# Second cross attention of a two-layer decoder: scores in half bursts, six turned tiles, the output product in four parts, late queries projected early

## The chip, the cores and the metric

The kernel runs on one core of one Trainium2 chip. The metric is the device time of one launch in microseconds; the time before is the median of three runs. The engines are TensorE (PE, with its weight loads PEld), VectorE (DVE), ScalarE (ACT), GpSimd (POOL) and SyncE (SP), which issues the loads. Each works through its own queue in order and meets the others only at semaphores.

## The reference

x is (8, 128, 512) in fp32 and passes six sublayers, each as `x = x + f(layernorm(x))`: a Taylor-like product with an FFN, a cross attention of 32 heads of 128, a LoRA FFN, a linear attention, the grouped cross attention that is changed here, and a 3-bit dequantised linear layer. The fifth is:

```
q = (queries @ Wq).reshape(b, s, KV_HEADS, GROUP, HEAD_DIM)     # 8 x 4 heads of 16
k = (keys @ Wk).reshape(b, s, KV_HEADS, HEAD_DIM)
v = (values @ Wv).reshape(b, s, KV_HEADS, HEAD_DIM)
scores = jnp.einsum('bqhgd,bkhd->bhgqk', q, k) * scale
attn = jax.nn.softmax(scores, axis=-1)
out = jnp.einsum('bhgqk,bkhd->bqhgd', attn, v).reshape(b, s, EMBED)
return out @ Wo
```

## The kernel before

Everything stays in SBUF between sublayers. Projections are written as three products of split operands (`mm3`, lines 542 to 544: high by high, low by high, high by low). The order on every engine is written out by hand.

The changed stage is the fifth sublayer. Its 8 batches times 8 key heads are worked in 16 groups n = 0 to 15 (`NG`), two per batch (b = n // 2, part = n % 2). A group has four tiles g = 0 to 3 (`KG`); each holds 4 heads of 128 queries by 128 keys, one PSUM bank of 128x512. Banks are sc0, sc1, pj0, pj1 for scores, tp and ou1 for turned tiles, pv for the heads' output and ou0 for projections and output products. For one group:

- `scores(n)` on PE (line 969): 8 matmuls with 32 rows each, tile g on rows 32g to 32g+31, so that four row groups work side by side.
- `row_max(n, g)` on DVE (line 1938), then `exps(n, g)` on ACT (line 1320, four ACTIVATEs), then `row_sums(n, g)` on DVE (lines 1945, 1948: a sum and a reciprocal), then `normalise` on POOL (line 514).
- `transposes(n, g)` on PE (line 983) turns the tile into tp or ou1; `turned_out(n, g)` on ACT (line 1329) copies it to `turned_whole` (`TW`, four tiles before).
- `values(n)` on PE (line 997) multiplies the four turned tiles with the values into pv. After the second group of a batch `heads(b)` takes pv to `act_hi` (ACT, line 1335) and `act_lo` (DVE, line 1954), `output(b)` on PE multiplies with Wo in four chunks (12 matmuls into ou0), and `add(b)` on DVE (lines 1397 and 1960) adds to x and takes the statistics.

`queries(hf, c)` projects four batches' queries for one of four column blocks: 12 matmuls into a bank and a copy on ACT (line 1312). Half 0 is done ahead of the groups. Half 1 goes through bank ou0 behind the groups 5, 6 and 7 (one, one and two blocks), because its result is written over that of half 0 in `act_whole` (`AF`).

`exps(n+1, g)` writes over the tile that `transposes(n, g)` reads (`PR[:, g]`). Before, ACT takes group n's turned tiles 0, 1 and 2 first and only then starts the exps of group n+1; `turned_out(n, ·)` waits for `values(n-1)`, since there are four turned tiles. DVE also has four parts of a dequantisation (`dequantise`, lines 1514 to 1518) for the last layer in its queue, ahead of group 0 and in groups 0, 1 and 3. POOL's order (`block_keys`, `pad_values`, four `normalise`) is not touched.

Of the kernel before, what the change touches and what calls it, by code (L numbers as in the profile page):

```python
# [17 lines left out]
FP32 = mybir.dt.float32  # L18
# [7 lines left out]
P = 128  # L26
# [63 lines left out]
NG = B * KVH // KG  # L90

# [17 lines left out]
def build(nc, a):  # L109
    ctx = ExitStack()  # L110
    with ctx:
# [33 lines left out]
        with ExitStack() as shared:  # L145
            TW = shared.enter_context(nc.sbuf_tensor("turned_whole", [P, KG, 512], FP32))
# [165 lines left out]
        query_banks = [ou[0], ou[1], pv, ou[0]]  # L312

# [224 lines left out]
        def _(pe):  # L538
# [398 lines left out]
            def queries(hf, c):  # L937
# [18 lines left out]
            def scores(n):  # L956

                b, part = n // 2, n % 2
                pe.wait_ge(kx_ready, n + 1)
                pe.wait_ge(q_out, b // HB * KC + 2 * part + 2)  # L960
                if n:
                    pe.wait_ge(lx_exp, n * KG)
                else:
                    pe.wait_ge(pj_done, PJ["ln4"] + B)
                for h in range(2):
                    for g in range(KG):
                        r = slice(32 * g, 32 * g + 32)
                        at = (2 * part + h) * HALF + b % HB * S
                        last = pe.matmul(score_banks[g][:, h * 256:(h + 1) * 256], AF[r, at:at + S], KX[r, n % 2, :],  # L969
                                         start=True, stop=True)  # L970
# [15 lines left out]
            def values(n):  # L986
# [8 lines left out]
                for g in range(KG):  # L995
                    at = part * P + 32 * g
                    last = pe.matmul(pv[32 * g:32 * g + 32, :], pads(b)[:, at:at + 32], TW[:, g, :],
# [3 lines left out]
            def output(b):  # L1001
                pe.wait_ge(on_done, b + 1)
                pe.wait_ge(x_done, OU["l1x"] + b)
                pe.wait_ge(q_out, 4 if b < 2 else 5 if b == 2 else 8)
                if b == 0:
                    ready(4, SLOT["l1x"][4])
                    ready(3, SLOT["l1x_o"])
                for c in range(KC):
                    last = mm3(ou[0][:], both(A, lambda t: t[:, ON1 + c * P:ON1 + (c + 1) * P]),
                               wrows(WO_SLOTS)(c), c == 0, c == KC - 1)  # L1010
                last.then_inc(ou_full, 1)
# [30 lines left out]
            scores(0)  # L1042
            queries(0, 3)
            for n in range(NG):
# [1080 lines left out]
```

## Time and profile before

| | |
|---|---|
| median of three runs | 2455.73 us (2455.06 to 2457.9) |
| the profiled execution: time, span | 2459.67 us, 2457.8 us |
| stage of the groups, first score to last `values` | 2266.4 to 2421.3 us of the span |
| PE, DVE, ACT, POOL busy in that stage of 154.9 us | 124.4, 114.6, 110.7, 78.0 us |

### The profile page before, as it was taken

To read this page: it belongs to the slowest core of one execution; us is meant where nothing else is said; L and a number is where in the kernel's file an instruction comes from. 1 tells how busy PE (TensorE), PEld (TensorE's weight loads), DVE (VectorE), ACT (ScalarE), POOL (GpSimd) and SP (SyncE) were. 2 spreads that over 40 slices of the span, in tenths; PEclk is the share of its full clock that TensorE was granted. 3 is DMA by queue.
4 is the path that set the end of the run, shared out by engine and by line. 5 is a ranking of instruction groups with operands and counts; after the bars stand their busy time and mean duration, and the time that the engine had idled before them with its cause. 6 is when DMAs were issued, how large, how long until landed. Compare 5 with 4: busy or idle time off the path is not lost.

```text
span 2457.8 us, 38454 instructions
## 1 busy us (share of the span) xinstructions
PE 2358.6 (96%) x13227; PEld 2012.9 (82%) x13227; DVE 1255.9 (51%) x2921; ACT 902.7 (37%) x2232; POOL 668.3 (27%) x383
## 2 busy tenths in 40 slices
PE   4999899999999999998999999999999999998788
PEld 3788688888888888987888888888888888887455
DVE  6444644444444444446554444444444444457766
ACT  2111344444444444443233333333333333334764
POOL 4334522322222232221231111111111111112542
PEclk9999999999999999999999999999999999999889
DMA  3110211211111111110111111111111111110000
GB/s 117 63 48 26 103 52 51 78 58 51 68 51 51 65 71 51 51 68 27 45 54 45 45 45 44 38 40 37 37 38 43 45 45 45 45 54 1 1 1 35
DMA packets 36832, 118.97 MB, mean 48 GB/s; under 512 B 4905, under 2 KB 7337, under 8 KB 36785
## 3 DMA queue, kind: packets, MB, share of 16 engines
q1 hardware_dynamic: 36784, 118.35, 14.1%
q8 instruction: 28, 0.46, 0.1%
q14 instruction: 20, 0.16, 0.0%
HBM read 116.24 MB, written 2.10 MB: 48 GB/s over the span
## 4 chain that ended last, share of the span: by engine, by line
PE 88%; DVE 5%; issue 3%; POOL 2%; ACT 1%; SPq 0%; DMA 0%; POOLq 0%; ACTq 0%; DVEq 0%
PE pj L542 19%; PE pj L543 19%; PE pj L544 19%; PE ou L542 6%; PE ou L544 6%; PE ou L543 6%; PE pv L720 2%; PE sc L857 2%; PE pv L866 2%; PE sc L704 2%; PE tp L711 1%; POOL w_lo L410 1%; POOL w_hi L408 1%; PE sc L969 1%; DVE neg_max L1938 1%
## 5 line engine op out<-in xcount | busy, mean ns | idle before, releaser
L402 POOL TENSOR_TENSOR w_lo<-raw,w_hi 128x1024 fp32r<-128x1024 f32 x145 | 346.7, 2391 | 1441.2 <-ACT w_hi L1104 1401.8
L542 PE MATMUL pj<-xt_hi,w_hi 128*128 128x512 f32 x1232 | 499.8, 406 | 6.6 <-DVE xt_lo L1473 2.4
L543 PE MATMUL pj<-xt_lo,w_hi 128*128 128x512 f32 x1232 | 483.1, 392 | 0.0
L544 PE MATMUL pj<-xt_hi,w_lo 128*128 128x512 f32 x1232 | 482.3, 392 | 0.0
L542 PEld LDWEIGHTS pj<-xt_hi,w_hi 128*128 128x128 f32 x1232 | 233.5, 190 | 51.1 <-issue 3.1
L542 PE MATMUL ou<-w_hi,act_hi 128*128 128x512 f32 x684 | 274.5, 401 | 0.8 <-DVE x L1397 0.6
L544 PEld LDWEIGHTS pj<-xt_hi,w_lo 128*128 128x128 f32 x1232 | 232.6, 189 | 49.7
L544 PE MATMUL ou<-w_hi,act_lo 128*128 128x512 f32 x684 | 267.6, 391 | 0.0
L543 PEld LDWEIGHTS pj<-xt_lo,w_hi 128*128 128x128 f32 x1232 | 233.6, 190 | 40.9
L543 PE MATMUL ou<-w_lo,act_hi 128*128 128x512 f32 x684 | 266.9, 390 | 0.0
L1397 DVE TENSOR_TENSOR x<-x,ou 128x512 f32<-128x512 f32 x192 | 130.8, 684 | 247.1 <-PE ou L544 246.8
L1255 ACT ACTIVATE side<-pj 128x512 f32<-128x512 f32 (+1 forms) x256 | 125.6, 491 | 341.1 <-PE pj L544 341.1
L1835 DVE TENSOR_TENSOR queries_keys<-side,pj 128x512 f32<-128x512 f32 x128 | 88.1, 688 | 184.6 <-ACT side L1255 184.6
L1170 ACT ACTIVATE queries_keys<-pj 128x512 f32<-128x512 f32 x128 | 76.5, 598 | 247.7 <-PE pj L544 247.7
L542 PE MATMUL pj<-w_hi,xt_hi 128*128 128x256 f32 (+1 forms) x544 | 160.8, 295 | 2.5 <-DVE x_sum L1475 1.6
L1104 ACT ACTIVATE w_hi<-raw 128x1024 fp32r<-128x1024 f32 x146 | 153.5, 1052 | 20.5 <-PE ou L544 18.7
L542 PEld LDWEIGHTS ou<-w_hi,act_hi 128*128 128x128 f32 x684 | 128.7, 188 | 36.6 <-issue 10.7
L544 PE MATMUL pj<-w_hi,xt_lo 128*128 128x256 f32 (+1 forms) x544 | 157.4, 289 | 0.0
L543 PE MATMUL pj<-w_lo,xt_hi 128*128 128x256 f32 (+1 forms) x544 | 157.3, 289 | 0.0
L544 PEld LDWEIGHTS ou<-w_hi,act_lo 128*128 128x128 f32 x684 | 128.7, 188 | 27.8
L543 PEld LDWEIGHTS ou<-w_lo,act_hi 128*128 128x128 f32 x684 | 129.0, 189 | 24.3
L542 PE MATMUL pj<-w_hi,ctx_hi 128*128 128x256 f32 x512 | 147.8, 289 | 0.7 <-POOL w_lo L410 0.7
(242 smaller groups left out, 4538.9 us busy)
## 6 DMA issues: line engine op xcount, KB each, us to landing
raw<-in_l1a_w SPq DMA_DIRECT2D x80, 512.0 KB, 4.1
raw<-in_l0x_w SPq DMA_DIRECT2D x64, 512.0 KB, 4.3
side<-in_side SPq DMA_DIRECT2D x32, 512.0 KB, 4.0
raw<-in_ffn_w SPq DMA_DIRECT2D x15, 512.0 KB, 3.3
raw<-in_l0f_w SPq DMA_DIRECT2D x6, 512.0 KB, 3.7
raw<-in_l1x_w SPq DMA_DIRECT2D x6, 512.0 KB, 3.8
raw<-in_taylor_w SPq DMA_DIRECT2D x5, 512.0 KB, 6.9
x<-in_x SPq DMA_DIRECT2D x2, 1024.0 KB, 6.4
```

The source lines that it names most:

```text
L402: pool.tensor_tensor(WL[:, s, :], RAW[:, s, :], f32(WH[:, s, :]), ALU.subtract).then_inc(w_ready[s], 1)
L542: pe.matmul(out, wh, xh, start=first, stop=False)
L543: pe.matmul(out, wh, xl, start=False, stop=False)
L544: return pe.matmul(out, wl, xh, start=False, stop=last)
L704: last = pe.matmul(score(j)[:, h * S:(h + 1) * S], heads_of(0, h, j), heads_of(1, h, j), start=True, stop=True)
L720: last = pe.matmul(pv[:, h * S:(h + 1) * S], VT[:, n, h * S:(h + 1) * S], TA[:, n % 2, h * S:(h + 1) * S], start=True, stop=True)
L857: last = pe.matmul(score(j)[:, h * S:(h + 1) * S], heads_of(1, h, j), heads_of(0, h, j), start=True, stop=True)
L1104: act.activation(WH[:, s, :], RAW[:, s, :], ACT.Copy).then_inc(w_hi[s], 1)
L1170: act.activation(QK[:, n, :], bank[:], ACT.Copy, scale=S ** -0.5 if n < 2 else 1.0).then_inc(pj_done, 1)
L1255: act.activation(F[:, x % 2, 0:w], pj[bank][:, 0:w], ACT.Sigmoid).then_inc(la_sg, 1)
L1397: dve.tensor_tensor(dst, dst, ou[bank][:], ALU.add).then_inc(x_done, 1)
L1835: dve.tensor_tensor(dst, F[:, x % 2, 0:w], pj[bank][:, 0:w], ALU.mult).then_inc(pj_done, 1)
```

## The change

`scores(n, two)` now issues the tiles 0 and 1, or 2 and 3: two bursts of 4 matmuls with two row groups each, each waiting for its own two exps of the group before. PE sends the first half of group n+1 ahead of `transposes(n, 0)` and the second behind `transposes(n, 1)`. `values(n-1)` moves into group n, behind its first turning. `TW` has six tiles (`NTW`), so `turned_out` waits for a `values` less often. `output(b)` is issued in four chunks: the first at the end of the even group 2b+2, the others in group 2b+3 between turnings. ACT alternates `exps(n+1, g)` and `turned_out(n, g)`. DVE takes `row_max(n+1, 0)` and `(n+1, 1)`, then `row_sums(n, 2)` and `(n, 3)`, then the other two maxima, then `row_sums(n+1, 0)` and `(n+1, 1)`. Half 1 of the queries goes to its own place (`RAWF`, two weight slots that are free by then), blocks 0 to 3 ahead of group 0, behind groups 0 and 1, and inside group 4. No instruction's shape changes, and the number of matmuls is the same.

```diff
+NTW = 6
-            TW = ... sbuf_tensor("turned_whole", [P, KG, 512], FP32))
+            TW = ... sbuf_tensor("turned_whole", [P, NTW, 512], FP32))
+        RAWF = RAW[:, 0:2, :].rearrange("p s n -> p (s n)")
+        QUERIES = [AF, RAWF]
...
-                if n in (4, 5):
-                    pe.wait_ge(x_done, OU["l1x"] + n - 2)
-                if n in (6, 7):
+                if n in (4, 5, 6):
                     pe.wait_ge(q_out, n)
+                if n == 7:
+                    pe.wait_ge(x_done, OU["l1x"] + 1)
...
-            def scores(n):
+            def scores(n, two):
                 b, part = n // 2, n % 2
-                pe.wait_ge(kx_ready, n + 1)
-                pe.wait_ge(q_out, b // HB * KC + 2 * part + 2)
+                if two == 0:
+                    pe.wait_ge(kx_ready, n + 1)
+                    pe.wait_ge(q_out, b // HB * KC + 2 * part + 2)
                 if n:
-                    pe.wait_ge(lx_exp, n * KG)
-                else:
+                    pe.wait_ge(lx_exp, (n - 1) * KG + 2 * two + 2)
+                elif two:
                     pe.wait_ge(pj_done, PJ["ln4"] + B)
                 for h in range(2):
-                    for g in range(KG):
+                    for g in (2 * two, 2 * two + 1):
...
             for n in range(NG):
+                late = n % 2 and n > 1
+                if n + 1 < NG:
+                    scores(n + 1, 0)
                 transposes(n, 0)
+                if n:
+                    values(n - 1)
+                if late:
+                    output(n // 2 - 1, (1,))
                 transposes(n, 1)
+                if n == 4:
+                    queries(1, 3)
                 if n + 1 < NG:
-                    scores(n + 1)
+                    scores(n + 1, 1)
+                if late:
+                    output(n // 2 - 1, (2,))
                 transposes(n, 2)
+                if late:
+                    output(n // 2 - 1, (3,))
                 transposes(n, 3)
                 if n % 2 == 0 and n:
-                    output(n // 2 - 1)
-                if n + 1 == NG:
-                    turned_weights(0)
-                    turned_weights(1)
-                values(n)
-                for c in {5: (0,), 6: (1,), 7: (2, 3)}.get(n, ()):
-                    queries(1, c)
+                    output(n // 2 - 1, (0,))
+                if n in (0, 1):
+                    queries(1, n + 1)
+            turned_weights(0)
+            turned_weights(1)
+            values(NG - 1)
...
             def turned_out(n, g):
                 t = n * KG + g
                 act.wait_ge(tn_full, t + 1)
-                if n:
-                    act.wait_ge(pg_full, n)
-                act.activation(TW[:, g, :], turn_banks[t % 2][:], ACT.Copy).then_inc(tn_out, 1)
+                if t >= NTW:
+                    act.wait_ge(pg_full, (t - NTW) // KG + 1)
+                act.activation(TW[:, t % NTW, :], turn_banks[t % 2][:], ACT.Copy).then_inc(tn_out, 1)
...
             for n in range(NG - 1):
+                exps(n + 1, 0)
                 turned_out(n, 0)
+                if n in (1, 2):
+                    queries(1, n)
+                exps(n + 1, 1)
                 turned_out(n, 1)
-                if n == 6:
-                    queries(1, 0)
+                if n % 2 == 0 and n:
+                    heads(n // 2 - 1)
+                exps(n + 1, 2)
                 turned_out(n, 2)
...
             for n in range(NG - 1):
-                for g in range(KG):
-                    row_max(n + 1, g)
+                row_max(n + 1, 0)
+                row_max(n + 1, 1)
+                row_sums(n, 2)
+                row_sums(n, 3)
+                row_max(n + 1, 2)
+                if n % 2 == 0 and n:
+                    heads(n // 2 - 1)
+                row_max(n + 1, 3)
                 if n in (0, 1, 3):
                     dequantise((0, 1, 3).index(n) + 1)
                 row_sums(n + 1, 0)
                 row_sums(n + 1, 1)
-                if n % 2 == 0 and n:
+                if n % 2 and n > 1:
                     add(n // 2 - 1)
...
```

**PE, an odd group.** Before, from the `values` of an even group to the `values` of the odd group behind it: pv is `values`, tp and ou from identity are the four turnings, sc and pj from `keys_blocked` the scores of the group that follows.

```order
L997 MATMUL pv<-turned_whole,values_padded 32x512 x4
L983 MATMUL tp<-identity,probs 128x128 x4
L983 MATMUL ou<-identity,probs 128x128 x4
L969 MATMUL sc<-keys_blocked,act_whole 128x256 x2
L969 MATMUL pj<-keys_blocked,act_whole 128x256 x2
...
L983 MATMUL tp<-identity,probs 128x128 x4
L983 MATMUL ou<-identity,probs 128x128 x4
L997 MATMUL pv<-turned_whole,values_padded 32x512 x4
```

After, the same group: sc and pj are the two half bursts, ou from `w_hi` and `w_lo` one chunk (three matmuls) of the output product.

```order
L974 MATMUL sc<-keys_blocked,raw 128x256 x4
L988 MATMUL tp<-identity,probs 128x128 x4
L1002 MATMUL pv<-turned_whole,values_padded 32x512 x4
L546 MATMUL ou<-w_hi,act_hi 128x512
L547 MATMUL ou<-w_lo,act_hi 128x512
L548 MATMUL ou<-w_hi,act_lo 128x512
L988 MATMUL ou<-identity,probs 128x128 x4
L974 MATMUL pj<-keys_blocked,raw 128x256 x4
...
L988 MATMUL tp<-identity,probs 128x128 x4
...
L988 MATMUL ou<-identity,probs 128x128 x4
```

The `values` product and a chunk now stand between the first and the second turning, so between the first turning and the second half of the next scores.

**ACT, the pass of an even group.** Before: `turned_whole` are the copies of turned tiles, `probs` the exps (x8 is two tiles).

```order
L1329 ACTIVATE turned_whole<-tp 128x512
L1329 ACTIVATE turned_whole<-ou 128x512
L1329 ACTIVATE turned_whole<-tp 128x512
L1320 ACTIVATE probs<-sc,neg_max 128x128 x8
L1329 ACTIVATE turned_whole<-ou 128x512
L1320 ACTIVATE probs<-pj,neg_max 128x128 x8
```

After, with `heads` (`act_hi` from pv) in it:

```order
L1339 ACTIVATE probs<-sc,neg_max 128x128 x4
L1348 ACTIVATE turned_whole<-tp 128x512
L1339 ACTIVATE probs<-sc,neg_max 128x128 x4
L1348 ACTIVATE turned_whole<-ou 128x512
L1354 ACTIVATE act_hi<-pv 128x512
L1339 ACTIVATE probs<-pj,neg_max 128x128 x4
L1348 ACTIVATE turned_whole<-tp 128x512
L1339 ACTIVATE probs<-pj,neg_max 128x128 x4
L1348 ACTIVATE turned_whole<-ou 128x512
```

The exps of the next group no longer stand behind three turned tiles of this one; `heads` moved from the odd group's pass to the next even group's, behind two exps and two copies.

On DVE, `heads` (`act_lo`) moved with it: it now has the maximum of tile 3, and so an exp, queued behind it, where before it stood between the last two row sums.

## Rows read from the trace of the kernel before

**Rows 1.** The page: span, and the granted clock in 40 slices.

```profile
span 2457.8 us, 38454 instructions
...
PEclk9999999999999999999999999999999999999889
```

**Rows 2.** Waits from 2266.4 to 2421.3 us: total, times, longest.

```profile
DVE neg_max L1938 <- PE pj L969: 24.8, 10, 7.9
...
PE pv L997 <- ACT turned_whole L1329: 19.2, 8, 2.8
```

**Rows 3.** DVE timeline, first row maxima of groups 1, 5, 9 and 15.

```profile
2277.58 1.29 DVE L1938 TENSOR_REDUCE neg_max<-sc 128x4 f32<-128x512 f32 x2 [1.10 <-PE pj L969]
...
2315.50 1.29 DVE L1938 TENSOR_REDUCE neg_max<-sc 128x4 f32<-128x512 f32 x2 [2.04 <-PE pj L969]
...
2358.98 1.29 DVE L1938 TENSOR_REDUCE neg_max<-sc 128x4 f32<-128x512 f32 x2 [7.92 <-PE pj L969]
...
2410.78 1.29 DVE L1938 TENSOR_REDUCE neg_max<-sc 128x4 f32<-128x512 f32 x2 [1.27 <-PE pj L969]
```

**Rows 4.** PE timeline, last late query to the values of group 9.

```profile
2354.00 0.50 PE L542 MATMUL ou<-xt_hi,w_hi 128*128 128x512 f32 x1 [0.69 <-ACT act_whole L1312]
...
2356.85 0.60 PE L983 MATMUL tp<-identity,probs 128*128 128x128 f32 x4
...
2357.82 0.48 PE L969 MATMUL sc<-keys_blocked,act_whole 32*128 32x256 f32 x2
...
2358.89 0.65 PE L983 MATMUL tp<-identity,probs 128*128 128x128 f32 x4
2359.38 0.60 PE L983 MATMUL ou<-identity,probs 128*128 128x128 f32 x4
2359.74 0.48 PE L542 MATMUL ou<-w_hi,act_hi 128*128 128x512 f32 x1
...
2362.78 1.06 PE L997 MATMUL pv<-turned_whole,values_padded 128*32 128x512 f32 x8
...
2370.34 1.94 PE L997 MATMUL pv<-turned_whole,values_padded 128*32 128x512 f32 x8 [2.24 <-ACT turned_whole L1329]
```

**Rows 5.** ACT timeline, group 9.

```profile
2367.14 0.60 ACT L1329 ACTIVATE turned_whole<-tp 128x512 f32<-128x512 f32 x1 [1.38 <-PE tp L983]
2367.63 2.17 ACT L1320 ACTIVATE probs<-sc,neg_max 128x128 f32<-128x128 f32 x8
...
2372.34 0.60 ACT L1335 ACTIVATE act_hi<-pv 128x512 fp32r<-128x512 f32 x1 [1.02 <-PE pv L997]
```

**Rows 6.** DVE timeline: a part of the dequantisation, then the add and two row sums.

```profile
2307.82 0.42 DVE L1514 TENSOR_SCALAR w<-w_bytes 128x512 f32<-128x512 uint8 x1
...
2309.61 0.68 DVE L1945 TENSOR_REDUCE row_sums<-probs 128x4 f32<-128x512 f32 x1
...
2363.09 0.66 DVE L1397 TENSOR_TENSOR x<-x,ou 128x512 f32<-128x512 f32 x1
...
2364.39 0.67 DVE L1945 TENSOR_REDUCE row_sums<-probs 128x4 f32<-128x512 f32 x1
...
2365.19 0.65 DVE L1945 TENSOR_REDUCE row_sums<-probs 128x4 f32<-128x512 f32 x1
```

**Rows 7.** POOL timeline, two tiles.

```profile
2365.35 2.04 POOL L514 TENSOR_TENSOR probs<-probs,row_recip 128x512 f32<-128x512 f32 x2 [0.97 <-DVE row_recip L1948]
```

**Rows 8.** Windows: length, busy PE, PEld, DVE, ACT, POOL, granted clock.

```profile
2366.20:2369.60 3.40, 1.31 (x8) 0.84 (x8) 3.24 (x6) 2.46 (x9) 1.76 (x3) 1.00 0.01 2
2369.60:2376.40 6.80, 6.06 (x33) 3.29 (x34) 3.57 (x9) 4.32 (x13) 4.53 (x5) 0.50 0.00 0
2376.40:2386.70 10.30, 8.31 (x60) 5.43 (x59) 9.73 (x19) 8.37 (x28) 5.37 (x8) 1.00 0.01 2
...
2359.00:2410.80 51.80, 42.99 (x277) 25.87 (x278) 40.61 (x82) 38.87 (x123) 28.55 (x33) 0.80 0.01 1
```

**Rows 9.** ACT and PE timelines: the last early query, the last values.

```profile
2270.70 0.60 ACT L1312 ACTIVATE act_whole<-ou 128x512 f32<-128x512 f32 x1 [0.72 <-PE ou L544]
...
2421.20 1.06 PE L997 MATMUL pv<-turned_whole,values_padded 128*32 128x512 f32 x8
```

More of the change, by code:

```diff
@@ L996, in values, with output @@
                     at = part * P + 32 * g
-                    last = pe.matmul(pv[32 * g:32 * g + 32, :], pads(b)[:, at:at + 32], TW[:, g, :],
+                    last = pe.matmul(pv[32 * g:32 * g + 32, :], pads(b)[:, at:at + 32], TW[:, (n * KG + g) % NTW, :],
                                      start=part == 0, stop=part == 1)
                 last.then_inc(pg_full, 1)
[L1001 to L1008, printed above, removed]
+            def output(b, chunks):
+                if chunks[0] == 0:
+                    pe.wait_ge(on_done, b + 1)
+                    pe.wait_ge(x_done, OU["l1x"] + b)
+                    pe.wait_ge(q_out, 8 if b else 7)
+                    if b == 0:
+                        ready(4, SLOT["l1x"][4])
+                        ready(3, SLOT["l1x_o"])
+                for c in chunks:
                     last = mm3(ou[0][:], both(A, lambda t: t[:, ON1 + c * P:ON1 + (c + 1) * P]),
                                wrows(WO_SLOTS)(c), c == 0, c == KC - 1)
-                last.then_inc(ou_full, 1)
+                if chunks[-1] == KC - 1:
+                    last.then_inc(ou_full, 1)
             def product(b):
@@ L1061, in _ @@
             turn(5, range(2))
-            output(B - 1)
+            output(B - 1, range(KC))
             for b in range(B):
@@ L1308, in queries @@
                 act.wait_ge(q_full, n + 1)
-                if hf:
-                    act.wait_ge(gs_full, (7 + c // 2) * KG)
                 bank = ou[0] if hf else query_banks[c]
-                act.activation(AF[:, c * HALF:(c + 1) * HALF], bank[:], ACT.Copy, scale=HD ** -0.5).then_inc(q_out, 1)
+                act.activation(QUERIES[hf][:, c * HALF:(c + 1) * HALF], bank[:], ACT.Copy, scale=HD ** -0.5).then_inc(q_out, 1)
             def exps(n, g):
@@ L1346, in _ @@
                 exps(0, g)
+            queries(1, 0)
             for n in range(NG - 1):
+                exps(n + 1, 0)
                 turned_out(n, 0)
+                if n in (1, 2):
+                    queries(1, n)
+                exps(n + 1, 1)
                 turned_out(n, 1)
-                if n == 6:
-                    queries(1, 0)
+                if n % 2 == 0 and n:
+                    heads(n // 2 - 1)
+                exps(n + 1, 2)
                 turned_out(n, 2)
-                exps(n + 1, 0)
-                exps(n + 1, 1)
+                if n == 4:
+                    queries(1, 3)
+                exps(n + 1, 3)
                 turned_out(n, 3)
-                exps(n + 1, 2)
-                if n % 2:
-                    heads(n // 2)
-                exps(n + 1, 3)
-                if n == 6:
-                    queries(1, 1)
-                if n == 7:
-                    queries(1, 2)
-                    queries(1, 3)
             turned_out(NG - 1, 0)
@@ L1964, in _ @@
                 row_max(0, g)
-            for g in range(KG):
-                row_sums(0, g)
+            row_sums(0, 0)
+            row_sums(0, 1)
             dve.wait_ge(w_hi[3], SLOT["l1x_o"] + 1)
@@ L1975, in _ @@
                 row_sums(n + 1, 1)
-                if n % 2 == 0 and n:
+                if n % 2 and n > 1:
                     add(n // 2 - 1)
-                if n + 2 == NG:
-                    half_deviation(5, 0)
-                row_sums(n + 1, 2)
-                if n % 2:
-                    heads(n // 2)
-                row_sums(n + 1, 3)
+            half_deviation(5, 0)
+            row_sums(NG - 1, 2)
+            row_sums(NG - 1, 3)
+            add(B - 2)
             def weights_lo(c):
```

11 lines of the change are left out of this document (6 added, 5 removed).

## The prediction

> **What bounds the kernel now.** The page first: PE is granted nearly its full clock, but 0.8 in two of the last three slices, 2273 to 2396 us [rows 1]. That is the changed stage, so only its 154.9 us are at stake. In the table of waits of this stage no engine is the bound: DVE waits for scores (24.8 us), PE for turned tiles (19.2 us) [rows 2]. It is a ring: scores, maximum, exps, sum, normalise, turn, copy, values, and back. The pace is best read from the first row maximum of a group: groups 1, 5, 9 and 15 begin at 2277.58, 2315.50, 2358.98 and 2410.78 [rows 3]. I call what lies between the first maximum of group n+1 and that of group n+2 pass n; it is pass n of the loops in the code. Passes 0 to 3 take 37.9 us, 4 to 7 43.5 us (they hold the late queries), 8 to 13 51.8 us, 17.3 us for each pair (one batch). From the maximum of group 15 to its values it is 2421.20 - 2410.78 = 10.4 us [rows 3, 9].
>
> Then the clock. In a stretch of 3.40 us PE works 1.31 us and waits; behind it the grant is 0.50 (1.2 GHz) for 6.8 us, in which a values product takes 1.94 us, where one at the full clock takes 1.06 [rows 4, 8]. Over passes 8 to 13 the mean grant is 0.80 [rows 8]. A fall stands behind the long wait (2.24 us for `turned_out`), once a pair.
>
> **Prices at the full clock.** All from starts in a row. PE [rows 4]: whole burst to the next turning 1.07 (2357.82 to 2358.89), and to the maximum that it releases 1.16 (2358.98 in [rows 3]); a turning 0.5; values 1.0; output product 3.04, so a chunk 0.76, which I take as 0.9 when it stands alone between others; a query block 2.85. ACT [rows 5]: copy 0.5, exps of a tile 1.0 (2.17 with its tail for two), `heads` 0.5. DVE: maximum 0.6 (1.29 with its tail for two [rows 3]); a row sum with its reciprocal 0.8 to 0.9, 0.89 taken; add and statistics 2364.39 - 2363.09 = 1.3; a dequantisation part 2309.61 - 2307.82 = 1.8 [rows 6]; `heads` 0.7, as other subtractions of this size. POOL: 1.0 a tile, with 0.1 to the turning [rows 7].
>
> A half burst is in no row. Its bounds are 0.43 (cost by the number of matmuls) and 0.86 in the array plus the 0.2 of a change of form (cost by the longest row group, since each row group still has the same matmuls in series). I take the upper one, 1.07 and 1.16, because four row groups ran side by side in the row. The Trainium skill says the same in "TensorEngine Tiling (Array Packing)", Theoretical Speedup: a dimension of 32 gives up to four times, which half bursts use half of, and by it PE's scores of a group double. By the lower bound instead the sum below would be some 3 us better.
>
> **An even pass after the change**, from its start at 0. DVE: two maxima to 1.2, two sums to 3.0, third maximum to 3.6. `heads` on DVE waits for ACT: exps from 0.7, copy, exps, copy to 3.7, `heads` done 4.3. DVE goes on to 5.0, last maximum 5.6, two sums 7.4. PE's first chunk and the next first half burst end before that (3.3 and 4.3 for the last turnings, chunk from 5.1, burst from 6.0, maximum possible at 7.15). So 7.4 us, 0.7 of it a wait that the moved `heads` makes.
>
> **An odd pass**, with 0 where the even one ends. The sum of tile 0 ended at -0.9; POOL is done with it at 0.3, turning 0.3, values 0.8 to 1.8, chunk to 2.7, second turning to 3.2, second half burst, third maximum at 4.4. DVE has been idle since 3.0. Then two maxima, two sums, the add: 4.4 + 1.2 + 1.8 + 1.3 = 8.7. A pair is 7.4 + 8.65 = 16.05 us (DVE alone has 14.0: eight maxima 4.8, eight sums 7.1, `heads` 0.7, add 1.3). PE is then idle for at most 1.1 us at a stretch in steady passes, so I take the full clock throughout.
>
> **The sum.**
> - Passes 8 to 13: 3 x 16.05 = 48.15 against 51.8: **-3.6**.
> - Start: the copy of query block 3 is done at 2271.2 (2270.70 + 0.5 [rows 9]). Late block 0 follows on PE to 2273.9, its scores give the first maximum at 2275.05 (2277.58 before). Passes 0 and 1 have a dequantisation on DVE and end in a query block on PE: sums to 3.0, POOL to 4.2, last turning 4.7, block to 7.5, scores 8.65 (DVE alone would need 7.8); pass 1 the same with 0.1 for the values, 8.8. Pass 2 is an even one whose `heads` is 0.5 later, behind the copy of a query block: 7.9. Pass 3 is an odd one with a dequantisation: 8.65 + 1.8. 2275.05 + 8.65 + 8.8 + 7.9 + 10.45 = 2310.85, against 2315.50: **-4.65**.
> - Passes 4 to 7: pass 4 has late block 3 between turning and half burst: it moves the third maximum from 3.0 to 5.4, and PE's first chunk waits for its copy, so 10.2; the others 8.65, 7.4, 8.65. Together 34.9 against 43.5: **-8.6**. Before, three of four query blocks stood bare in passes 5 to 7 (behind the last two DVE had been idle for 7.9 us [rows 3]); now their passes are the ones that DVE's dequantisations fill.
> - The end: before, one output product was over before the last group's turnings, now three chunks stand between them, and they don't overlap with scores any more. From the last maximum of [rows 3]: 7.7 turning, values 9.2, chunk and turning 10.6, chunk 11.5, turning, chunk 12.9, turning 13.4, weights' turnings, values at 14.4 against 10.4: **+4.0**. Behind it the same work follows as before.
> - The larger `TW`, the other place for queries and the waits that are left out add no instruction: 0. Their cover is that ACT has 12.4 us of work in a pair (eight exps 8, eight copies 4, `heads` 0.5); without it an exp's start would move, but DVE sets the pace.
>
> -3.6 - 4.65 - 8.6 + 4.0 = -12.9 us. The profiled execution took 2459.67 us, its span 2457.8, which would become 2444.9; the median of the runs is 3.9 below that time, and -12.9 from 2455.73 gives **2442.8 us**.
>
> **The rivals.** I call no change what lies within 0.2% (4.9 us), about what a measurement of this kernel can tell.
>
> 1. *The low clock comes back, and PE now stands in the ring (ends slower).* In an odd pass, turning, values, chunk, turning and half burst lie one behind the other, 0.5 + 1.0 + 0.9 + 0.5 + 1.16 = 4.1 us, and at 0.50 of the clock 7.8. A fall in each of seven pairs costs 7 x 3.7 = 26 us and gives 2469; it decides at the fourth (12.9 / 3.7 = 3.5). For it: gaps remain (0.9 and 0.5 between turnings in an even pass, up to 1.1 behind a half burst). Against: the fall in the rows stands behind a wait of 2.24 us and one stretch of 3.40 us with 1.31 busy, and the 10.3 us with PE busy 8.31 kept their clock [rows 4, 8]; the new passes have 12 of 16 us busy. One to three falls: 2446 to 2454, 13 in 100; four or more: 2457 to 2469, 14 in 100. The Trainium skill speaks for it in "TensorE: Matmul & The Clock Gate", A second HAM failure mode: frequent small idle spells between groups of matmuls make the clock oscillate. The trace agrees so far that the clock of this stage swings.
> 2. *Little of it arrives.* At the full clock the old order is not much worse: its even leg (9.8 us) would be 8.3 with the 1.5 us of slow values, turnings and scores taken out, so a pair 15.9. What the new order gives is a kept clock and hidden queries. If handoffs that I laid back to back slip by 0.5 us in every pass, 15 x 0.5 takes 7.5 us back: 2450. Between 2450.8 and 2460 for this reason: 7 in 100.
> 3. *The ring opens further.* If a half burst costs 0.43 and the chunk hides, only DVE is left: 14.0 a pair, 2 us better on seven pairs, 2429. Unlikely, since `heads` waits for ACT however fast PE is: 6 in 100.
> 4. The forecast, 2437 to 2449: 60 in 100.
>
> **How the numbers follow.** Forecast and rival 3 and most of the light form of rival 1 are faster by over 0.2%: 0.74. Within 0.2%: the rest of it, rival 2, and the beginning of the heavy form: 0.14. Slower: 0.12. The range of 8 in 10 leaves out rival 3's lower part and the heavy form of rival 1: 2435 to 2456.
>
> **What would show it.** Right: the first maximum of group 15 near 2394, pairs of 16 us, granted clock near 1.0 in the stage, a DVE wait for `act_hi` of 0.7 in even passes and one for scores of 1.4 in odd ones, the last values 14 us behind the maximum. A half burst's eight records would have four starts 0.21 us apart. Wrong: a grant of 0.50 in odd passes, pairs above 17.3, or PE waiting over 2 us for turned tiles.

## The result: 0.4% faster, near the forecast

| | median (lowest to highest, runs) | ratio to before, 95% interval |
|---|---|---|
| before | 2457.69 us (2455.06 to 2459.61, 9) | |
| changed | 2448.02 us (2439.76 to 2450.17, 9) | 0.9959 (0.9949 to 0.9969) |
| forecast | 2442.8 us (2435 to 2456) | 0.9947 |

The ratio makes 10.1 us, where -12.9 was worked out. The changed kernel is faster by more than 0.2%, and its time lies inside the range. Its profiled execution took 2446.26 us. The page of the changed kernel, to be held against [rows 1]: no slice has an 8 left.

```profile
span 2443.8 us, 38448 instructions
...
PEclk9999999999999999999999999999999999999999
```

The DVE timeline of the changed kernel, first maxima of groups 1, 5, 9 and 15, which answer to [rows 3]. Passes 0 to 3 lie between the first two, 4 to 7 between the next two, 8 to 13 before the last.

```profile
2271.38 1.29 DVE L1955 TENSOR_REDUCE neg_max<-sc 128x4 f32<-128x512 f32 x2 [1.09 <-PE sc L974]
...
2308.81 1.27 DVE L1955 TENSOR_REDUCE neg_max<-sc 128x4 f32<-128x512 f32 x2
...
2346.16 1.27 DVE L1955 TENSOR_REDUCE neg_max<-sc 128x4 f32<-128x512 f32 x2
...
2393.68 1.27 DVE L1955 TENSOR_REDUCE neg_max<-sc 128x4 f32<-128x512 f32 x2
```

The first maximum of group 0 stands at 2268.12 before and at 2264.16 after:

```profile
2268.12 1.28 DVE L1938 TENSOR_REDUCE neg_max<-sc 128x4 f32<-128x512 f32 x2
...
2264.16 1.28 DVE L1955 TENSOR_REDUCE neg_max<-sc 128x4 f32<-128x512 f32 x2
```

These 4.0 us don't come from the change. The maximum follows DVE's own queue without a wait in both kernels, and the distance is already there in the layernorm ahead of it (its `var_eps` at 2257.14 and 2253.18). Profiled executions of kernels whose code is the same up to there have the maximum anywhere from 2264.2 to 2268.1. So all sums below run from the first maximum of group 0 to the end of the span: 189.68 us before, 179.64 after, 10.0 less, where the ratio makes 10.1. Each is one execution, so that the two agree so closely is partly chance.

| stretch, us | before | changed | difference | forecast |
|---|---|---|---|---|
| first maximum of group 0 to that of group 1 | 9.46 | 7.22 | -2.2 | |
| passes 0 to 3 | 37.92 | 37.43 | -0.5 | -4.65 with the line above |
| passes 4 to 7 | 43.48 | 37.35 | -6.1 | -8.6 |
| passes 8 to 13 | 51.80 | 47.52 | -4.3 | -3.6 |
| last first maximum to the end of the span | 47.02 | 50.12 | +3.1 | +4.0 |

The windows of the changed kernel with the columns of [rows 8]: the stage, three stretches around its two clock falls, and passes 8 to 13.

```profile
2264.10:2407.60 143.50, 126.20 (x771) 78.08 (x774) 110.84 (x230) 108.71 (x336) 78.75 (x92) 0.96 0.00 1
2290.70:2297.50 6.80, 5.17 (x33) 3.25 (x34) 5.36 (x13) 6.33 (x20) 4.42 (x7) 1.00 0.00 1
2297.50:2300.90 3.40, 3.40 (x14) 1.31 (x13) 2.13 (x6) 1.63 (x5) 2.63 (x3) 0.50 0.02 5
...
2314.50:2317.90 3.40, 1.41 (x9) 0.82 (x7) 2.99 (x7) 3.09 (x11) 1.05 (x2) 1.00 0.00 0
2317.90:2324.70 6.80, 6.80 (x26) 3.58 (x26) 2.81 (x6) 2.16 (x7) 3.48 (x4) 0.50 0.00 0
...
2346.20:2393.70 47.50, 42.64 (x276) 25.65 (x276) 39.05 (x83) 39.26 (x124) 29.36 (x37) 1.00 0.01 1
```

Before, passes 8 to 13 had a mean grant of 0.80 [rows 8]; now it is 1.00. Over the stage the granted clock was 0.50 (1.2 GHz) for some 51 us before, summed over short windows, and for 10.2 us after. The table of waits of this stage, 2262 to 2408 us, against [rows 2]: DVE's wait for scores stands in two rows now, 18.2 and 5.4 us, together 23.6 where it was 24.8, so it hardly shrank and only comes in shorter pieces (3.3 at the longest, where it was 7.9). What shrank is PE's wait for turned tiles, from 19.2 to 2.6 us (0.5 at the longest, where it was 2.8).

```profile
DVE neg_max L1955 <- PE pj L974: 18.2, 14, 3.3
...
PE tp L988 <- POOL probs L518: 6.8, 8, 1.6
...
DVE neg_max L1955 <- PE sc L974: 5.4, 4, 2.5
...
PE pv L1002 <- ACT turned_whole L1348: 2.6, 5, 0.5
```

A steady pair in the changed kernel, on PE: the odd pass of group 9 (its second turning, second half burst, next chunk).

```profile
2355.41 0.50 PE L546 MATMUL ou<-w_hi,act_hi 128*128 128x512 f32 x1
...
2356.22 0.60 PE L988 MATMUL ou<-identity,probs 128*128 128x128 f32 x4
2356.75 1.13 PE L974 MATMUL pj<-keys_blocked,raw 32*128 32x256 f32 x8
2357.81 0.50 PE L546 MATMUL ou<-w_hi,act_hi 128*128 128x512 f32 x1
```

A half burst takes 2357.81 - 2356.75 = 1.06 us in the array, as a whole one did (1.07 in [rows 4]). On DVE the two waits that were forecast in a pair:

```profile
2350.56 0.69 DVE L1971 TENSOR_TENSOR act_lo<-pv,act_hi 128x512 fp32r<-128x512 f32 x1 [0.46 <-ACT act_hi L1354]
...
2357.91 1.29 DVE L1955 TENSOR_REDUCE neg_max<-pj 128x4 f32<-128x512 f32 x2 [1.66 <-PE pj L974]
```

An even pass is 7.21 us long and an odd one 8.63, a pair 15.84; 7.4, 8.65 and 16.05 were forecast.

### The profile page after: what moved, and what is told of

Same layout as the page of the kernel before. It is cut to its first block, busy times and chain, and to the rows that moved or that the text cites. A ratio compares the mean times of both kernels' runs of the same rounds, so it can differ in the third digit from the quotient of the medians.

```text
span 2443.8 us, 38448 instructions
## 1 busy us (share of the span) xinstructions
PE 2360.0 (97%) x13227; PEld 2012.1 (82%) x13227; DVE 1254.2 (51%) x2921; ACT 902.4 (37%) x2232; POOL 669.2 (27%) x383
## 4 chain that ended last, share of the span: by engine, by line
PE 88%; DVE 5%; issue 2%; POOL 2%; ACT 1%; SPq 0%; DMA 0%; POOLq 0%; ACTq 0%; DVEq 0%
PE pj L546 19%; PE pj L547 19%; PE pj L548 19%; PE ou L546 6%; PE ou L548 6%; PE ou L547 6%; PE pv L724 2%; PE sc L861 2%; PE pv L870 2%; PE sc L708 2%; PE tp L715 1%; POOL w_lo L414 1%; POOL w_hi L412 1%; DVE neg_max L1955 1%; DVE probs L1455 1%
```

## The experiments

Eleven kernels were run, each in several rounds beside the kernel before (2457.71, 2456.97 and 2455.97 us on the three chips). All stretches are taken from the starts of first maxima in one profiled execution each, from the first maximum of group 0 to the end. "Low" is the time at a granted clock of 0.50 in the stage of that execution. The ratio is the comparison with the runs of the kernel before on the same chip, and not the quotient of the medians shown (the two differ by up to 0.0009). The changed kernel was not run again beside the eleven, so it and they meet only through the kernel before; differences between two kernels below are differences of their ratios, times 2457 us.

| kernel | median us | ratio, 95% | 0 to 1 | passes 0-3 | 4-7 | 8-13 | last to end | sum | low |
|---|---|---|---|---|---|---|---|---|---|
| before | 2457.69 | | 9.46 | 37.92 | 43.48 | 51.80 | 47.02 | 189.68 | 51 |
| changed | 2448.02 | 0.9959 (0.9949-0.9969) | 7.22 | 37.43 | 37.35 | 47.52 | 50.12 | 179.64 | 10 |
| queries only | 2447.46 | 0.9963 (0.9949-0.9976) | 8.32 | 40.13 | 34.72 | 48.16 | 46.06 | 177.39 | 24 |
| queries late | 2454.49 | 0.9995 (0.9986-1.0004) | 6.05 | 38.49 | 42.75 | 47.54 | 51.60 | 186.43 | 20 |
| whole bursts | 2457.40 | 1.0002 (0.9993-1.0011) | 7.45 | 40.41 | 38.39 | 50.91 | 52.13 | 189.29 | 34 |
| output whole | 2452.10 | 0.9977 (0.9967-0.9986) | 7.23 | 36.82 | 39.39 | 51.35 | 48.92 | 183.71 | 10 |
| four tiles | 2449.52 | 0.9966 (0.9952-0.9979) | 7.22 | 37.40 | 38.56 | 47.50 | 51.73 | 182.41 | 17 |
| before + filler | 2452.03 | 0.9982 (0.9973-0.9991) | 9.48 | 36.79 | 40.69 | 46.58 | 49.29 | 182.83 | 24 |
| changed + filler | 2445.79 | 0.9961 (0.9948-0.9975) | 7.22 | 35.85 | 34.76 | 47.50 | 51.45 | 176.78 | 3 |
| block 3 earlier | 2444.03 | 0.9956 (0.9942-0.9969) | 7.23 | 39.07 | 31.64 | 47.49 | 50.69 | 176.12 | 0 |
| chunks later | 2444.68 | 0.9955 (0.9942-0.9969) | 7.22 | 36.62 | 34.96 | 46.37 | 51.79 | 176.96 | 10 |
| combined | 2441.63 | 0.9943 (0.9930-0.9957) | 7.22 | 38.32 | 33.16 | 46.40 | 48.98 | 174.08 | 7 |
| queries + filler | 2440.36 | 0.9936 (0.9922-0.9950) | 8.30 | 37.32 | 33.29 | 46.80 | 47.72 | 173.43 | 7 |

**Queries only.** The order of before on every engine, and only the late query blocks moved: block 0 ahead of group 0, 1 and 2 behind groups 0 and 1, 3 behind group 4.

```diff
+            queries(1, 0)
             for n in range(NG):
...
                 values(n)
-                for c in {5: (0,), 6: (1,), 7: (2, 3)}.get(n, ()):
+                for c in {0: (1,), 1: (2,), 4: (3,)}.get(n, ()):
                     queries(1, c)
```

> The order of before, with only the late queries taken from it: their own place, blocks 0 to 3 ahead of group 0 and behind groups 0, 1 and 4. If the queries are the largest term, as in my sum (passes 4 to 7 and the start), this alone gives 5 to 8 us against before, and pairs of groups stay at 17.3 us with the low clock in them. If the half bursts and the alternating exps are what hides the queries (rival), the blocks stand bare here too and it gives 0 to 3 us.

Measured 2447.46 us, 0.9963: the whole gain of the change as far as the intervals tell (9.1 us against 10.1), with none of its new order, and more than the 5 to 8 us expected, since the pairs did not stay at 17.3 us (48.16 us for three, 16.05 each). This was the surprise of the study. The windows of this kernel for groups 1 to 4, 4 to 9 and passes 8 to 13:

```profile
2277.00:2306.00 29.00, 23.77 (x152) 15.57 (x152) 21.36 (x45) 20.19 (x63) 13.96 (x19) 0.88 0.01 2
2306.00:2351.10 45.10, 34.79 (x240) 22.71 (x236) 34.77 (x70) 33.51 (x104) 24.75 (x31) 0.89 0.00 1
2351.10:2399.30 48.20, 38.32 (x281) 23.82 (x277) 40.72 (x81) 39.09 (x123) 29.65 (x37) 0.93 0.01 1
```

In steady pairs the old order keeps its clock in one pair of three (0.93 in the mean, where [rows 8] have 0.80): the legs with a fall take 9.09 and 8.96 us, the one without 8.18. By stretches the queries bring -1.1 before the passes, +2.2 in passes 0 to 3, -8.8 in 4 to 7, and -3.6 in 8 to 13. What differs from before in these passes is only what went ahead: their instructions come in the same order, only 7.8 us sooner and with the queries read from the other place, and yet they last 48.16 us instead of 51.80. So the falls there are not fixed by the order, and "17.3 us a pair" was not a property of the order alone. Whether what went ahead decides them, or only the single execution, these two profiles don't tell; for the former speaks that all five runs of this kernel have a mean grant of 0.990 to 0.992, and the 20 runs of the kernel before beside them 0.986 to 0.989.

**Queries late.** The reverse: the changed kernel, whose late blocks come late again (block 0 inside group 4, the others inside group 6).

```diff
-                if n == 4:
-                    queries(1, 3)
+                for c in {4: (0,), 6: (1, 2, 3)}.get(n, ()):
+                    queries(1, c)
...
-                if n in (0, 1):
-                    queries(1, n + 1)
```

> The changed kernel with its late query blocks late again: one inside group 4, three inside group 6, none ahead. What the half bursts, six tiles and four parts give alone. The start gains 3 us a block in passes 0 and 1 (about 1 each, since DVE sets the pace there) and 2.9 ahead of group 0's successor, pass 6 pays 3 x 3.5 = 10.5: 3 to 7 us slower than the changed kernel, 2451 to 2455. If the queries' place did not matter (rival): within 2 us of the changed kernel.

Measured 0.9995: the new order by itself is worth nothing that this measurement can tell, although passes 8 to 13 are as short as in the changed kernel (47.54). The DVE timeline of this kernel shows the price of three bare blocks in one pass:

```profile
2340.02 0.69 DVE L1948 TENSOR_REDUCE neg_max<-pj 128x4 f32<-128x512 f32 x1 [10.56 <-PE pj L973]
```

The third maximum waits 10.56 us for scores that stand behind the blocks; that pass has 16.83 us. It is a harder placement than that of before, which spread the blocks over three passes, so the order alone may be worth more than this figure; that was not measured. By the ratios this kernel is 8.8 us slower than the changed one, where 3 to 7 was expected.

**Whole bursts.** The changed kernel with one burst for all four tiles where the first half burst stood; it must wait for all four exps of the group before.

```diff
-                    pe.wait_ge(lx_exp, (n - 1) * KG + 2 * two + 2)
+                    pe.wait_ge(lx_exp, n * KG)
...
-                    for g in (2 * two, 2 * two + 1):
+                    for g in range(KG) if n else (2 * two, 2 * two + 1):
...
-                if n + 1 < NG:
-                    scores(n + 1, 1)
```

> The changed kernel with whole bursts again, each at the place of the first half, so that it waits for all four exps. My prices: the second half burst leaves the odd pass's chain (1.1 us less there), but the burst waits for the last exp, about 1 us later in each pass: 15 x 0.5 to 1.0, 5 to 15 us slower than the changed kernel. The rival, that the half bursts' double array time eats what they free: 0 to 5 us faster than the changed kernel.

Measured 1.0002: without half bursts nothing of the gain is left, 10.6 us more than the changed kernel. PE at the head of group 12, and the window of passes 8 to 13:

```profile
2384.92 0.48 PE L974 MATMUL sc<-keys_blocked,raw 32*128 32x256 f32 x2 [1.93 <-ACT probs L1337]
```
```profile
2351.80:2402.70 50.90, 37.71 (x280) 22.61 (x276) 38.91 (x81) 39.06 (x123) 29.38 (x36) 0.97 0.00 1
```

PE waits 1.93 us for the last exp at the head of a pass, and turning, values and chunks queue behind it. Falls are back over the stage (34 us low), but passes 8 to 13 have only one: the pairs are 17.0 us long at a mean grant of 0.97, so there most of it is a wait and not the clock. A whole burst behind the second turning, where the kernel before has it, was not tried in the new order.

**Output whole.** All four chunks at the end of the even group.

```diff
-                late = n % 2 and n > 1
+                late = False
...
-                    output(n // 2 - 1, (0,))
+                    output(n // 2 - 1, (0, 1, 2, 3))
```

> The changed kernel with the output product in one piece at the end of the even pass. The odd pass loses 0.9 us of its chain (third maximum 0.8 earlier), the even one gets 2.3 us on PE between the last turning and the next scores: first maximum at 5.1 + 3.0 + 1.2 = 9.3 instead of 7.2. A pair 15.8 + 2.1 - 0.8 = 17.1, seven pairs +9 us; the end gains 2 us. So 5 to 9 us slower than the changed kernel. The rival, that the four parts only lengthen the odd chain: 0 to 5 us faster.

Measured 2452.10 us, 4.4 more than the changed kernel, a little under the 5 to 9 expected. Odd passes fall to 7.33 us, even ones rise to 9.26 and more, since the next first half burst stands behind 3.0 us of output. DVE, first maximum of group 6, the worst place:

```profile
2327.64 1.29 DVE L1955 TENSOR_REDUCE neg_max<-sc 128x4 f32<-128x512 f32 x2 [5.18 <-PE sc L974]
```

The end is 1.2 us shorter (48.92 to 50.12), since three chunks no longer stand between the last turnings.

**Four tiles.** `NTW = 4` in the changed kernel.

```diff
-NTW = 6
+NTW = 4
```

> The changed kernel with four turned tiles. The copy of tile 0 now waits for the values product behind the first turning, 1.1 us later than with six; on ACT the second exps stand behind it. ACT has slack in odd passes (three waits of 0.7 to 1.0 us before exps) but heads stands behind it in even ones: 0.5 us a pair, 2 to 5 us slower than the changed kernel. If six tiles do nothing: the same within 2 us.

Measured 2449.52 us, 1.7 more than the changed kernel, with intervals that overlap for the most part. Passes 8 to 13 are the same to 0.02 us. The profile has pass 4 at 13.32 instead of 11.22, with one more fall at its start, and another fall behind the last first maximum (51.73 us to the end, where it was 50.12). Inconclusive.

**Before with filler.** The kernel before with two unused matmuls (128x512, into ou0) behind the last turning of each odd group from 3 on, where PE waited for the turned tiles. They compute nothing that is used.

```diff
+                if n % 2 and n > 1:
+                    pe.wait_ge(x_done, OU["l1x"] + (n - 1) // 2)
+                    if n == 7:
+                        pe.wait_ge(q_out, 6)
+                    for _ in range(2):
+                        pe.matmul(ou[0][:], IDN[:], BIAS[:], start=True, stop=True)
```

> The kernel before with extra work on PE: in every odd pass from group 3, two matmuls of 128x512 (identity by a constant) into the free bank of the output product, between the last turning and the values, where PE waits 2.24 us. Their result is written over and not used. If the low clock costs the old order 1.5 us a pair, as I worked out, it stays at 1.0 there and seven pairs give 5 to 10 us. If the clock's fall is hidden by other waits, or the extra work costs what it saves: within 2 us of before, or slower by up to 6.

Measured 2452.03 us, 0.9982: extra work makes the kernel before 4.4 us faster, where 5 to 10 was expected. The window of its passes 8 to 13:

```profile
2353.30:2399.90 46.60, 40.54 (x291) 23.95 (x289) 40.47 (x81) 39.09 (x123) 27.75 (x33) 1.00 0.00 1
```

The grant is 1.00 and a pair takes 15.5 us, less than the new order at the same clock (15.84). In group 15 part of this is lost: 49.29 us to the end, where it was 47.02. There the filler stands bare ahead of the last values, in a stretch of 3.4 us at the low clock that the kernel before did not have.

**Changed with filler.** The changed kernel with a 128x256 matmul behind the first half burst of odd groups and two of 128x512 in group 4, again unused.

```diff
+                if late and n + 1 < NG:
+                    pe.wait_ge(on_done, (n - 1) // 2)
+                    pe.matmul(pv[:, 0:256], IDN[:], BIAS[:, 0:256], start=True, stop=True)
...
+                if n == 4:
+                    pe.wait_ge(on_done, 2)
+                    for _ in range(2):
+                        pe.matmul(pv[:], IDN[:], BIAS[:], start=True, stop=True)
```

> The changed kernel with the same kind of extra work, not used: 256 columns between the first half burst and the first turning of odd passes, and twice 512 behind the last turning of pass 4, where its trace has a wait of 2.0 us and then the low clock. The low clock of passes 3 to 5 cost about 4 us against my sum; kept, the kernel gains 2 to 5 us on the changed one, and its runs spread less than 2440 to 2450. If the falls are not what made those passes long: the same or 1 to 2 us slower.

Both falls of the changed kernel are gone from its profile: from group 3 to the last values the mean grant is 0.99, with one short fall behind the last maximum.

```profile
2290.00:2405.00 115.00, 104.72 (x655) 63.33 (x652) 89.53 (x188) 89.16 (x274) 65.61 (x79) 0.99 0.01 1
```

Passes 3, 4 and 5 take 10.42, 10.38 and 8.56 us, where the changed kernel had 11.98, 11.22 and 10.29: 4.1 us for two falls. The forecast had 10.45, 10.2 and 8.65. But the ratio (0.9961) is not apart from 0.9959, where a gain of 2 to 5 us was expected: that the filler helps the kernel's time is not shown, only that this execution has no falls in these passes. It has 1.3 us more behind the last first maximum (51.45 to 50.12), where its one fall stands, and its mean grant of 0.998 is the highest of its five runs; the others have 0.995 and 0.996.

**Block 3 earlier.** The changed kernel with late block 3 behind group 1 together with block 2, and the copies of both at the end of ACT's pass 1.

```diff
-                if n == 4:
-                    queries(1, 3)
...
+                if n == 1:
+                    queries(1, 3)
```

> The changed kernel with the last late query block moved from inside group 4 to behind group 1, at the end of that pass. Passes 4 and 5 lose 2.6 + 1.7 us (they took 11.2 and 10.3), pass 1 gets 3.6 (block and copy): 1 to 4 us faster than the changed kernel if the place of the block made the wait of 2.0 us and the low clock behind it; if the block costs its 2.9 us wherever it stands: the same within 1.

Passes 4 and 5 become plain ones, 7.18 and 8.63 us, no fall at all is left from group 0 to the last values, and pass 1 pays:

```profile
2265.70:2405.00 139.30, 122.07 (x767) 76.02 (x766) 110.64 (x229) 108.71 (x336) 78.74 (x92) 1.00 0.00 1
```
```profile
2294.46 1.29 DVE L1954 TENSOR_REDUCE neg_max<-sc 128x4 f32<-128x512 f32 x2 [4.58 <-PE sc L972]
```

Pass 1 has 12.69 us instead of 8.99. The sum of this execution is 3.5 us shorter than in the changed kernel, the ratio lower by 0.0003 only (0.7 us, where 1 to 4 was expected); the two are not apart.

**Chunks later.** The changed kernel with chunks 1, 2 and 3 each one turning later, so that none stands between the values and the second turning.

```diff
-                if late:
-                    output(n // 2 - 1, (1,))
                 transposes(n, 1)
...
                 if late:
-                    output(n // 2 - 1, (2,))
+                    output(n // 2 - 1, (1,))
                 transposes(n, 2)
```

> The changed kernel with each late chunk of the output product one turning later, so that between the first turning and the second half burst only the values product stands. By my ring the third maximum of an odd pass comes 0.8 us sooner and the pair takes 15.0 instead of 15.84: seven pairs, 4 to 6 us faster than the changed kernel. If another wait takes its place (the exps of tile 1, or the last chunk ahead of the next scores): 0 to 2 us faster.

The second half burst moves up by 0.7 us in the odd pass, and half of that arrives: 8.27 instead of 8.63. Where the rest goes stands on DVE:

```profile
2354.81 1.29 DVE L1955 TENSOR_REDUCE neg_max<-pj 128x4 f32<-128x512 f32 x2 [0.91 <-PE pj L974]
...
2357.97 0.69 DVE L1414 TENSOR_TENSOR x<-x,ou 128x512 f32<-128x512 f32 x1 [0.28 <-PE ou L548]
```

The wait for scores is 0.91 instead of 1.66, but the add now waits 0.28 for the last chunk. A pair is 15.46 us, as the filled old order has it, and not 15.0 as expected: another wait took the place. The ratio (0.9955) is not apart from the changed kernel's.

**Combined.** Block 3 earlier, chunks later, and the output product of batch 6 whole at the end of group 14, so that group 15 has none between its turnings.

```diff
-                late = n % 2 and n > 1
+                late = n % 2 and 1 < n < NG - 1
...
-                    output(n // 2 - 1, (0,))
+                    output(n // 2 - 1, (0,) if n < NG - 2 else range(KC))
```

> The changed kernel with three moves: the last late query block behind group 1, each late chunk one turning later, and the output product of the last batch but one in one piece at the end of group 14's pass. From the traces of its parts: passes 8 to 13 in 46.4 us, 4 to 7 in 31 us, the end 3 us shorter. 170 to 172 us from the first row maximum to the end, against 179.6 in the changed kernel: 2438 to 2441 us if the clock stays up; 2 to 4 us more if it falls once or twice.

Measured 2441.63 us, 3.9 below the changed kernel, with intervals that overlap in part. The end takes 48.98 us; of the 3.1 us that the new end cost, 1.1 came back, where 3 was expected. From the first maximum of group 0 to the end there are 174.08 us, 2 more than the 170 to 172 expected, with one stretch of 6.8 us at the low clock in it.

**Queries with filler.** The kernel "queries only" with two unused matmuls behind the last turning of odd groups, group 15 left out.

```diff
+                if n % 2 and n + 1 < NG:
+                    pe.wait_ge(q_out, {1: 6, 3: 7}.get(n, 8))
...
+                    for _ in range(2):
+                        pe.matmul(ou[0][:], IDN[:], BIAS[:], start=True, stop=True)
```

> The order of before with early queries, and extra work on PE (two 128x512 matmuls, not used) behind the last turning of odd groups but the last. If the clock is what the new order gives in steady passes, the old order with a kept clock needs nothing else: passes 8 to 13 in 46.6 us as with extra work alone, the stage 172 to 175 us, 2441 to 2444 us, faster than the changed kernel by 4 to 7. If half bursts and alternating exps give more than the clock, it stays at 2447 or above.

Measured 2440.36 us (2436.07 to 2442.06), the best of all, in the order of before. PE in pass 11 (the last turning of group 11, the filler, the values), and the window of passes 8 to 13:

```profile
2368.25 0.66 PE L985 MATMUL ou<-identity,probs 128*128 128x128 f32 x4 [0.34 <-POOL probs L516]
2368.74 1.88 PE L1061 MATMUL ou<-bias,identity 128*128 128x512 f32 x4
2371.14 1.06 PE L999 MATMUL pv<-turned_whole,values_padded 128*32 128x512 f32 x8 [0.52 <-ACT turned_whole L1336]
```
```profile
2343.90:2390.70 46.80, 40.48 (x292) 23.95 (x288) 40.61 (x81) 39.20 (x123) 29.62 (x37) 1.00 0.00 1
```

The 1.9 us of filler lie in the wait for turned tiles, of which 0.52 are left; nothing is behind them that would have been earlier. That is slightly better than the 2441 to 2444 expected. It and "combined" (2441.63) are not apart from each other. Against the changed kernel it is 5.7 us better, and the intervals just touch (0.9950 and 0.9949).

## Why the prediction was right, and where it was wrong

**Right in the total, which owes something to luck.** The sum is off by 2.8 us of 12.9: the start and passes 4 to 7 gained 1.9 and 2.5 us less than worked out, the steady passes gained 0.7 more and the end cost 0.9 less. The falls that were left out fit into the range, and what follows shows that the reason given for one term was wrong.

**Right in the price of a half burst.** 1.06 us against 1.07: here the cost follows the longest row group, not the number of matmuls. The Trainium skill's "TensorEngine Tiling (Array Packing)", Theoretical Speedup, gives up to four times for a dimension of 32; the trace agrees, since a burst with two row groups takes as long as one with four. The kernel buys its earlier start with twice the array time, and "whole bursts" shows that inside this order it is worth it against a whole burst at the first half's place.

**Right in the steady passes.** 7.21 and 8.63 us against 7.4 and 8.65. The wait of `heads` on DVE is 0.46 and not 0.7, that for scores in the odd pass 1.66 and not 1.4, and a chunk stands bare between values and second turning (2356.22 - 2355.41 = 0.81 against 0.9). -4.3 us against -3.6.

**Wrong: "so I take the full clock throughout".** This is the step that failed, and rival 1 in its light form came true. In front of the fall at 2297.5 us PE worked 5.17 of 6.80 us, with no wait above 0.6 us (0.57 for a copied tile at the longest). The fall at 2317.9 stands behind a wait that pass 4 makes itself, as the PE timeline of the changed kernel shows: its first chunk waits for the copy of query block 3, which on ACT stands behind an exp and a copy.

```profile
2293.65 0.63 PE L988 MATMUL ou<-identity,probs 128*128 128x128 f32 x4 [0.57 <-ACT turned_whole L1348]
...
2298.20 1.94 PE L1002 MATMUL pv<-turned_whole,values_padded 128*32 128x512 f32 x8
...
2317.06 0.47 PE L546 MATMUL ou<-w_hi,act_hi 128*128 128x512 f32 x1 [1.99 <-ACT raw L1331]
...
2317.93 2.08 PE L974 MATMUL sc<-keys_blocked,act_whole 32*128 32x256 f32 x8
...
2320.98 1.94 PE L1002 MATMUL pv<-turned_whole,values_padded 128*32 128x512 f32 x8
```

I had that wait in the sum as a length and did not ask what it does to the clock; "PE is then idle for at most 1.1 us at a stretch" was said of steady passes, and applied to all. "Changed with filler" puts the price of the two falls at 4.1 us, 1.6 for the one of 3.4 us (pass 3) and 2.6 for the one of 6.8 (passes 4 and 5), and not 3.7 each. At half the clock 10.2 us can lose at most 5.1 us of PE's work, so most of it arrives; that the rest falls where the ring doesn't wait for PE is argued and not shown. Without falls, in "changed with filler", passes 4 to 7 take 34.76 us, which is -8.7 against before, where -8.6 was forecast.

**Wrong in size: the start.** -2.7 us against -4.65. The fall in pass 3 (11.98 in place of 10.45) is 1.5 of the gap; passes 0 to 2 took 8.78, 8.99 and 7.68 us, where 8.65, 8.8 and 7.9 were worked out. Another 0.3 lies ahead of them: the late query block and its lead to the scores took 2.95 us (2267.27 to 2270.22), where the sum left 2.7 (2271.2 to 2273.9), less than its own price of 2.85.

**The end: +3.1 in place of +4.0.** The last values stand 13.8 us behind the last first maximum against 10.4, +3.4 where +4.0 was worked out, and what follows them is 0.3 shorter.

```profile
2407.50 1.07 PE L1002 MATMUL pv<-turned_whole,values_padded 128*32 128x512 f32 x8
```

**Wrong in its reason, though not in its number: what gives the 3.6 us of the steady pairs.** I wrote in rival 2 that the old order at the full clock would have 15.9 us a pair, and still put the term down to the new order. Its long leg there was misread too: passes 9, 11 and 13 of the kernel before take 10.02, 10.11 and 9.98 us and not 9.8, and with the clock kept ("before with filler") 8.19, 8.23 and 8.24; the low clock cost 1.7 us a pair (51.80 against 46.58 for three) and not 1.5. (DVE's 14.0 us a pair, by the terms beside it, is 13.9.) Measured, the old order has 15.5 and 15.6 (46.6 and 46.8 us for three pairs in the two filled kernels, filler included) and the new one 15.84. So at one clock the new order is the slower of the two by about 0.3 us a pair, and all of the gain in these passes is the kept clock.

Over the whole stage, "queries only" has the full gain and "queries late" none. What the change brings comes from two things, the query blocks that went where DVE had its dequantisations, and a clock that falls less often. Moving the query blocks alone brings part of the second too (24 us low instead of 51); the new order brings it in the steady passes whatever went ahead (no fall in passes 8 to 13 of "queries late" either, 47.54 us), and pays for it with 3 us at the end and 0.3 a pair. That the new order keeps the clock by shorter waits is argued from the windows and the table of waits; that the clock and not the order decides the pairs is shown by the filled kernels.

**What stays open.** Why the fall at 2297.5 came at all: the same sequence of half bursts, turnings and chunk ran in passes 8 to 13 without one. It stands behind pass 2, in which ACT also copies a query block. The profiles of "four tiles" and "chunks later" have it there too; those of "block 3 earlier" and "combined", where that copy moved to the end of pass 1, don't, and in "block 3 earlier" PE worked 5.70 of the 6.80 us in the same place. "Output whole" and "changed with filler" have the copy in pass 2 and no fall there, with more for PE to do around it. That points at the copy, but with one execution each it is not shown. The nine runs of the changed kernel have mean grants of 0.995 (six runs, 2447.5 to 2450.2 us), 0.997 (two, 2445.7 and 2446.3) and 0.998 (one, 2439.8), so the falls of the profiled execution are not those of every run; what sets their number was not found. It was not tried either how much of the 10.6 us of "whole bursts" is its clock.

## What to carry to other kernels

Compare two orders of a ring at the same granted clock before crediting either: here a few unused matmuls in the longest wait of the old order were worth at least as much as the rewritten one, and told apart what order and clock each gave. Undo each part and do each part alone: the smallest edit of the change (four query blocks moved to passes in which another engine is busy anyway) carried the whole gain. When a sum contains a wait of PE of 2 us, put the clock's price beside it at once: here such a wait (1.99 us) had 6.8 us at the low clock behind it.

## What the runs showed of the hardware that was not expected

- A fall of the clock came behind a stretch of 6.80 us with PE busy for 5.17 and no wait above 0.6 us (changed kernel, 2290.7 to 2297.5), while 47.5 us with PE busy 42.64 kept the full clock. The Trainium skill's page "TensorE: Matmul & The Clock Gate", A second HAM failure mode, describes a clock that swings when PE idles briefly and often between groups of matmuls; the trace agrees for the first stretch, and the second shows that small gaps alone don't always bring it about.
- More work made the kernel before faster: 14 matmuls that nobody reads, six of them in passes 8 to 13, took these passes from 51.80 to 46.58 us and the ratio to 0.9982 (0.9973 to 0.9991).
- The same order of instructions, entered 7.8 us sooner in one profiled execution each, lost the clock in two pairs of three and more briefly, instead of in every one ("queries only", passes 8 to 13: a mean grant of 0.93 against 0.80).
- Two falls with 10.2 us at the low clock between them cost 4.1 us, most of the 5.1 us of PE's work that half the clock can lose in them (an estimate from these lengths).
